# A graph network on one core: normalised nodes turned chunk by chunk, three PSUM banks for the sums of three edge loops, lane numbers in a bank

## The chip, the cores and the metric

One core of a Trainium2 chip runs the whole program in one launch. The metric is the device time of that launch in microseconds, median of several executions. Engines are written as in the profile: PE multiplies matrices (PEld loads its weights), DVE and ACT work on whole tiles, POOL issues the indirect gathers and scatters here, SP issues the plain transfers.

## The reference

A graph of N = 6250 nodes with 128 features and E = 100,000 edges (`src` to `dst`, sorted by `dst`) goes through four layers, each followed by a residual and a layer norm:

```python
x = layernorm(x + conv(x))         # silu(h[src] + edge_attr @ we.T + be) summed by dst, silu, graph norm
x = layernorm(x + attend(x))       # h = x@W+b; e = leaky_relu(a_src.h[src] + a_dst.h[dst]); softmax over
                                   # all edges; weight * h[dst] summed by src
x = layernorm(x + heads(x))        # 8 heads of 16: clip(K[src].Q[dst]/4, -5, 5), exp, softmax per dst,
                                   # V[src] * weight summed by dst
x = layernorm(x + update(x))       # relu([x[src], x[dst], edge_attr] @ w1 + b1) @ w2 + b2 summed by dst,
                                   # then an MLP of [x, sum] with 256 hidden
```

Everything is float32.

## The kernel before, in words

Nodes lie as 50 tiles of 128 (NT; 49 of them, RT, hold real nodes), edges as tiles of 128. Since edges are sorted by `dst`, the edge tiles are walked in 832 steps of one edge tile and one node tile each; a step's sum by `dst` is a matmul with a one-hot matrix (edge by place in the node tile), and what an edge takes from its `dst` node is a matmul with that matrix transposed. What it takes from its `src` node is gathered from a table in DRAM by POOL, one indirect transfer for 128 edges.

The program is a row of stages, each a block in which every engine has its own instruction stream, written by hand. PSUM is one tile of 8 banks of 128x512 floats (`k.psum[:, bank, :]`). `pipeline(eng, iters, per, *stages, lags=...)` (line 79) emits an engine's loop: stage s of turn t - lag(s), one after the other, so the order of the names is the order of issue on the engine.

*conv* (`phase_conv_edges`, 585): not touched. DVE's comparison of line 705 to 708 reads its lane numbers from PSUM.

*Node stages.* Three stages begin with a layer norm of all nodes and a linear layer on it. `Norm` (494) does it in three cuts of tiles, 12, 20 and 18: DVE makes a cut's input (`make`), takes statistics (`count`, `moments`), ACT takes the root (`scalar_root`), DVE finishes (`finish`), then 4, 6 and 10 tiles of the cut are scaled by DVE (`apply`, 538) and the rest by ACT (`scalar_apply`, 550). `Linear` (401) takes chunks of 4 tiles (3 in place): PE turns a chunk (line 435), once all scaling of its cut is done on both engines, ACT copies it out (456), PE multiplies (442), DVE adds the bias into the result (472, or 474 with a scale), SP stores it in the table in DRAM (480). Products of at most `RING = 3` chunks are under way. In heads there are two layers on the same turned nodes, key and value (256 columns, 13 chunks) and query (128 columns); in relation also two, source and target (256 columns each). POOL's gathers begin when the first one's table is stored.

*Place* (`phase_place`, 852) has 104 groups of 8 steps, two buffers (j). Per group ACT makes |lo - p| (`distance`, 997) and from it the one-hot `is_lo` (`is_nought`, 1002); DVE makes `is_rel` by a comparison (`matrices`, 1082, line 1085) and a mask (`make_mask`, 1087). PE ranks the edges (`place`), scores them (`score`, 963 and 964) and fetches their rows of H (`expand`, 968, line 973) into banks 4 + 2j + h, 4 of the 8 steps each. ACT copies those to SBUF (1012). POOL scatters each step's rows into the DRAM table by_src (1157).

*Heads* (`phase_heads`, 1300) has 208 groups of 4 steps. POOL gathers key and value rows (1352) when DVE has staged the indices (`stage`, 1424). ACT makes the transposed one-hot (1393 to 1405), PE expands the query (`expand`, 1364), DVE multiplies with the key (1453), sums by head (1463), clips (1466). ACT takes the exponential into 8 columns of the message tile (`weigh`, 1408, line 1412), DVE multiplies the value rows by it (`messages`, 1470, line 1472) and stages the next indices. PE sums (`sum_into_nodes`, 1375, line 1381) with the one-hot of `sum_matrix` (1447, line 1449: lane numbers in PSUM bank 7) and DVE adds the sums into the nodes (1491).

*Relation* (`phase_relation`, 1499) has 208 groups of 4 steps. POOL gathers (1568), PE makes the hidden layer in banks 0 to 3 (`hidden_product`, 1582, lines 1590 and 1591), DVE adds the gathered rows in two halves (`add_rows`, line 1680) and stages the next indices, ACT takes Relu (1631), PE sums into banks 4 to 7 (`sum_into_nodes`, 1596, line 1602) with the one-hot that DVE makes in two comparisons (`sum_matrix`, 1666, line 1669: lane numbers in SBUF), DVE adds the four sums (`add_sums`, 1691, line 1701). The bank of a sum is 4 + 2(j mod 2) + q // 2. PE's order is hidden product of a group, sum of two groups back. DVE's order and the bank formula are:

```python
sums = lambda j, q: k.psum[:, 4 + 2 * (j % 2) + q // 2, (q % 2) * HID:(q % 2 + 1) * HID]
pipeline(v, ITERS, GROUPS, add_sums(0), sum_matrix, add_sums(1), add_rows(0), add_sums(2),
         add_rows(1), add_sums(3), lags=(3, 1, 3, 1, 3, 1, 3), loads=3)
```

The stage *attend* between place and heads and the stage *update* after relation are not touched (update has a norm of its own making with other code).

## Time and profile before

| | |
|---|---|
| median of 3 runs | 6345.29 us (6343.44 to 6368.28) |
| profiled execution | 6365.66 us, span 6363.8 us |
| TensorE clock granted, mean of the span | 0.742 of full speed |
| PE, PEld | 4055.2 us busy (64%), 3547.0 (56%) |
| DVE | 2974.2 us (47%) |
| ACT | 1648.3 us (26%) |
| POOL | 3414.5 us (54%) |
| HBM | 554.38 MB read, 89.82 MB written, 101 GB/s over the span |

The stages in the profiled execution, in us from the span's start: tables to 91, conv's loop 91 to 1408, graph norm and place's node stage to 1524, place's loop 1524 to 2890, attend to 3183, heads' node stage 3183 to 3272 (its key and value part to 3242), heads' loop to 4685, relation's node stage to 4793, relation's loop to 6224, update to the end. A busy share is an average over these stages, so the prediction reads each by itself. An entry such as "[7.13 <-remote]" behind an instruction is the idle time of its engine just before it and what ended that time: a line of another engine, "issue" where the profile shows nothing that was waited for, or "remote" for a semaphore that did not come from an engine's instruction in the records next to it.

### The profile page before, as it was taken

How to read it: one execution, taken by the hardware profiler on the slowest of the kernel's cores; microseconds unless marked ns; L12 is line 12 of the kernel's file. 1: busy time of each engine (PE TensorE's matmuls, PEld its weight loads, DVE VectorE, ACT ScalarE, POOL GpSimd, SP SyncE). 2: the span in 40 equal slices, each digit the busy share in tenths (PEclk: the TensorE clock that was granted, in tenths of full speed). 3: DMA queues.
4: the chain of work that ended last, by engine and by line, in shares of the span. 5: the costliest groups of instructions: out<-in, count | busy, mean ns of one | idle time of the engine just before them, and what ended most of it. 6: DMA issues, size and time to landing. Idle time of an engine off the chain costs nothing. (4 is left out here: it accounts for less than half of the span.)

```text
span 6363.8 us, 91532 instructions
## 1 busy us (share of the span) xinstructions
PE 4055.2 (64%) x19917; PEld 3547.0 (56%) x19918; DVE 2974.2 (47%) x8069; ACT 1648.3 (26%) x2977; POOL 3414.5 (54%) x3536
## 2 busy tenths in 40 slices
PE   4444444456888888787844333344458888888887
PEld 3444444445777777776743333344346677667765
DVE  5444444455333333336755555455464444445455
ACT  0111111113222222226732222222223333333331
POOL 3655555542566656566635555555524555555550
PEclk6766766775555555558977777766678999999999
DMA  4322222235222222226633333333324444444441
GB/s 103 85 81 81 80 79 79 80 77 99 80 80 83 82 79 81 80 74 183 194 99 97 95 98 95 97 95 95 98 93 121 132 132 133 133 136 137 130 131 49
DMA packets 491156, 645.54 MB, mean 101 GB/s; under 512 B 94519, under 2 KB 354059, under 8 KB 490798
## 3 DMA queue, kind: packets, MB, share of 16 engines
q1 hardware_dynamic: 346462, 312.02, 18.0%
q0 software_dynamic: 132032, 325.99, 17.7%
q10 hardware_dynamic: 12560, 6.52, 0.7%
q14 instruction: 82, 0.67, 0.0%
q8 instruction: 20, 0.33, 0.0%
HBM read 554.38 MB, written 89.82 MB: 101 GB/s over the span
## 5 line engine op out<-in xcount | busy, mean ns | idle before, releaser
L1568 POOL DMA_INDIRECT R<-table_ps,r_idx x832 | 805.5, 968 | 730.4 <-DVE r_idx L1642 393.1
L1352 POOL DMA_INDIRECT R<-table_kv,h_idx x832 | 804.0, 966 | 693.5 <-DVE h_idx L1424 383.4
L1157 POOL DMA_INDIRECT by_src<-R,p_idx x832 | 825.1, 992 | 631.9 <-issue 245.7
L626 POOL DMA_INDIRECT R<-table,c_idx x784 | 747.4, 953 | 560.1 <-DVEq L721 284.8
L1381 PE MATMUL psum<-R,h_oh 128*128 128x137 f32 x1664 | 338.8, 363 | 809.8 <-DVE R L1491 745.7
L658 PE MATMUL psum<-R,c_oh 128*128 x1664 | 351.0, 376 | 691.4 <-remote 237.5
L1381 PEld LDWEIGHTS psum<-R,h_oh 128*128 128x128 f32 x1664 | 292.5, 254 | 840.2 <-DVE R L1491 759.9
L658 PEld LDWEIGHTS psum<-R,c_oh 128*128 128x128 f32 x1664 | 299.5, 270 | 740.8 <-issue 740.8
L1701 DVE TENSOR_TENSOR R<-R,psum 128x256 f32 x832 | 343.6, 413 | 727.8 <-remote 437.4
L1590 PE MATMUL psum<-w_L_gnn_re_w,r_ea 128*128 128x256 f32 x1664 | 549.2, 413 | 188.4 <-DVE X L1680 170.6
L973 PE MATMUL psum<-R 128*128 x1664 | 438.0, 426 | 183.4 <-issue 178.9
L1591 PE MATMUL psum<-R 128*128 x1664 | 537.3, 405 | 19.2 <-issue 19.1
L739 DVE TENSOR_TENSOR R<-R,psum 128x128 f32 x832 | 238.6, 287 | 577.3 <-remote 301.2
L973 PEld LDWEIGHTS psum<-R 128*128 128x128 f32 x1664 | 381.8, 323 | 222.6 <-issue 222.3
L1590 PEld LDWEIGHTS psum<-w_L_gnn_re_w,r_ea 128*128 128x128 f32 x1664 | 336.4, 207 | 273.2 <-issue 224.5
L963 PE MATMUL psum<-p_src_score,R 128*128 128x50 f32 x1664 | 467.9, 374 | 19.8 <-issue 19.5
L1602 PE MATMUL psum<-X,early_cols 128*128 128x256 f32 x1664 | 411.3, 389 | 18.6 <-issue 15.4
L668 ACT ACTIVATE R<-R 128x512 f32<-128x512 f32 x196 | 123.4, 629 | 1146.1 <-DVE R L717 885.5
L964 PE MATMUL psum<-R 128*128 x1664 | 399.2, 307 | 27.9 <-issue 27.4
L1631 ACT ACTIVATE X<-X 128x1024 f32<-128x1024 f32 x208 | 219.9, 1057 | 754.4 <-DVE X L1680 645.2
L963 PEld LDWEIGHTS psum<-p_src_score,R 128*128 128x128 f32 x1664 | 380.6, 280 | 51.4 <-issue 51.0
L964 PEld LDWEIGHTS psum<-R 128*128 128x128 f32 x1664 | 387.5, 285 | 20.1 <-issue 19.9
(338 smaller groups left out, 7440.5 us busy)
## 6 DMA issues: line engine op xcount, KB each, us to landing
R<-by_src SPq DMA_DIRECT2D x220, 260.0 KB, 3.1
r_ea<-in_ea_t SPq DMA_DIRECT2D x832, 64.0 KB
R<-in_ea_t SPq DMA_DIRECT2D x196, 256.0 KB
R<-rel_rows SPq DMA_DIRECT2D x104, 256.0 KB
R<-lo_rows SPq DMA_DIRECT2D x104, 256.0 KB
h_rel<-rel_rows SPq DMA_DIRECT2D x208, 128.0 KB
r_rel<-rel_rows SPq DMA_DIRECT2D x208, 128.0 KB
by_src<-R,p_idx POOLq DMA_INDIRECT x832
```

The costliest lines, as they stand in the source:

```text
L626: g.indirect_dma_start(out=rows[:, u, :], out_offset=None, in_=table, in_offset=bass.IndirectOffsetOnAxis(ap=idx[:, j // GROUPS % 2, u:u + ...
L658: mm = pe.matmul(k.psum[:, 2 + j % 2, q * D:(q + 1) * D], oh[:, j % 2, q, :], ring[:, bass.ds(regs["slot"][G * (j % GROUPS) + q], 1), :], ...
L963: pe.matmul(cols[:, 0:NT], is_lo[:, j, q * P:(q + 1) * P], src_score[:], start=True, stop=True)
L964: mm = pe.matmul(cols[:, NT:WIDE], is_rel[:, j, q * P:(q + 1) * P], H[:, bass.ds(regs["node"][G8 * j + q], 1), D + 1:D + 2], start=True, s ...
L973: mm = pe.matmul(k.psum[:, 4 + 2 * j + h, (q % G) * D:(q % G + 1) * D], is_rel[:, j, q * P:(q + 1) * P], H[:, bass.ds(regs["node"][G8 * j ...
L1157: g.indirect_dma_start(out=by_src, out_offset=bass.IndirectOffsetOnAxis(ap=idx[:, u:u + 1], axis=0), in_=rows[:, u, :], in_offset=None).th ...
L1352: g.indirect_dma_start(out=rows[:, u, :], out_offset=None, in_=table, in_offset=bass.IndirectOffsetOnAxis(ap=idx[:, u:u + 1], axis=0)).the ...
L1381: mm = pe.matmul(sums(j, q), oh[:, j % 2, q, :], msg[:, j % 2, q, :], start=True, stop=True)
L1568: g.indirect_dma_start(out=rows[:, u, :], out_offset=None, in_=table, in_offset=bass.IndirectOffsetOnAxis(ap=idx[:, u:u + 1], axis=0)).the ...
L1590: pe.matmul(hidden(j, q), ea[:, G * j + q, :], k.w["L3_gnn_re_w1"][:, 2 * HID:3 * HID], start=True, stop=False)
L1591: mm = pe.matmul(hidden(j, q), oht[:, j % 2, q * P:(q + 1) * P], Dh[:, bass.ds(regs["node"][G * j + q], 1), :], start=False, stop=True)
L1602: mm = pe.matmul(sums(j, q), oh[:, j % 2, q, :], msg[:, j % 2, q, :], start=True, stop=True)
```

## The change

It has five parts.

1. *Linear.* The ring of products under way is 6 banks divided by the banks of a chunk: 6 chunks in place and for the query, 3 elsewhere. Sums of the first `on_scalar` chunks can be plain copies by ACT (`scalar_moves`), counted by a semaphore of their own; whoever waits for a sum asks `wait_sums`. `sums` gives, for each point of DVE's order in the norm, up to which chunk it has made the sums.
2. *Norm.* Scaling goes by the linear layer's chunks: DVE takes 1 tile of each chunk in place and heads, 2 in relation, ACT the rest, and each signals per chunk; PE turns a chunk when that chunk is scaled. The cuts become 15, 21, 14 in place and 16, 20, 14 in relation (heads 12, 20, 18 as before). In relation ACT makes the first 7 sums of the source layer, whose bias is zero. `make` comes in two steps. DVE's sums start earlier in its order in place and heads.
3. *Place's loop.* ACT makes `is_rel` too, by the two activations it uses for `is_lo`; the distances of both have one buffer. `expand` has three banks: the first half of both j goes to bank 4, the second to 5 or 6; it waits for one more copy. Bank 7 holds lane numbers, set by one matmul, and the mask is made from it.
4. *Heads' loop.* The exponential is taken twice: into PSUM bank 6, from where the messages read it, and then into the message tile. Waits move with it.
5. *Relation's loop.* The sums have three banks: q = 0 and 1 of every group use bank 4, q = 2 and 3 bank 5 or 6; PE's sum waits for the first two adds of the group before. Bank 7 holds lane numbers, and each group has one comparison.

The core of the diff:

```diff
+        self.ring = 6 // self.banks
...
+    def wait_sums(self, eng, n):
+
+        if n < self.on_scalar:
+            eng.wait_ge(self.moved, n + 1)
+        else:
+            eng.wait_ge(self.added, n - self.on_scalar + 1)
...
-            pe.wait_ge(self.norm.done, self.norm.cut_of(at + t - 1) + 1)
-            pe.wait_ge(self.norm.scaled, self.norm.cut_of(at + t - 1) + 1)
+            pe.wait_ge(self.norm.scaled, n + 1)
+            if self.norm.on_vector:
+                pe.wait_ge(self.norm.done, n + 1)
...
-            if n >= self.RING:
-                pe.wait_ge(self.added, n - self.RING + 1)
+            if n >= self.ring:
+                self.wait_sums(pe, n - self.ring)
...
+    def scalar_moves(self, a, upto):
+        for n in range(self.scalar_sums, min(upto, self.on_scalar)):
+            first, t = self.chunks[n]
+            a.wait_ge(self.product, n + 1)
+            for at in range(0, t, self.fit):
+                m = min(self.fit, t - at)
+                ins = self.nc.scalar.copy(self.OUT[:, first + at:first + at + m, :],
+                                          self.k.psum[:, self.bank(n, at), 0:m * self.cols].rearrange("p (t d) -> p t d", d=self.cols))
+            ins.then_inc(self.moved, 1)
+            self.scalar_sums = n + 1
...
+        last = len(self.cuts) - 1
         for n, cut in enumerate(self.cuts):
+            make(cut, 0)
             if n:
                 self.finish(link, v, n - 1)
+                self.apply_chunks(v, Y, OUT, n - 1, linear)
+                linear.vector(v, sums[2 * n - 2])
+            make(cut, 1)
+            self.count(v, Y, cut.start, cut.stop).then_inc(self.counted, 1)
             self.moments(link, v, n)
-        self.finish(link, v, len(self.cuts) - 1)
+            if n:
+                linear.vector(v, sums[2 * n - 1])
...
+        for n, (at, t) in enumerate(linear.chunks):
+            if at in [cut.start for cut in self.cuts]:
+                self.scalar_root(a, self.cut_of(at))
+                linear.scalar_copies(a, n)
+                linear.scalar_moves(a, n - 1)
+                a.wait_ge(self.known, self.cut_of(at) + 1)
+            for tile in range(at + min(self.on_vector, t - 1), at + t):
+                ins = self.nc.scalar.activation(OUT[:, tile, :], Y[:, tile, :], ACT.Identity, bias=self.shift[:, tile:tile + 1],
+                                                scale=self.root[:, tile:tile + 1])
+            ins.then_inc(self.scaled, 1)
+            linear.scalar_copies(a, n)
+            linear.scalar_moves(a, n - 1)
+        linear.scalar_copies(a, linear.count)
+        linear.scalar_moves(a, linear.count)
...
+        norm = Norm(nc, c, sem, "n0_", (slice(0, 15), slice(15, 36), slice(36, NT)), 1)
...
+        expand_bank = lambda j, h: 4 + h * (1 + j)
...
-                        pe.wait_ge(rows_ready, 2 * n + h + 1)
+                        pe.wait_ge(rows_ready, 2 * n + 3 - h)
...
+                def distances(i, j):
+                    n = PER * i + j
                     a.wait_ge(lo_in[j], 16 * i + 16)
+                    a.wait_ge(lo_ready, n + PER)
+                    nc.scalar.activation(lo_away, lo[:, j, :], ACT.Abs, bias=k.minus_part[:, 0:1]).then_inc(lo_used, 1)
+                    a.wait_ge(rel_in[j], 16 * i + 16)
+                    if not (isinstance(n, int) and n < 1):
+                        a.wait_ge(rel_ready, n)
+                    nc.scalar.activation(rel_away, rel[:, j, :], ACT.Abs, bias=k.minus_part[:, 0:1]).then_inc(rel_used, 1)
+
...
-                def matrices(i, j):
-                    v.tensor_scalar(is_rel[:, j, :], rel[:, j, :], k.part[:, 0:1], None, ALU.is_equal).then_inc(rel_used, 1)
...
+                    pe.wait_ge(kept, n + 3)
...
+                    a.wait_ge(msg_ready, n + GROUPS)
+                    nc.scalar.activation(share, score[:, j % 2], ACT.Exp).then_inc(weighed, 1)
                     a.wait_ge(spread, n + 1)
-                    nc.scalar.activation(msg[:, j % 2, :, D:D + HEADS], score[:, j % 2], ACT.Exp).then_inc(weighed, 1)
+                    nc.scalar.activation(msg[:, j % 2, :, D:D + HEADS], score[:, j % 2], ACT.Exp).then_inc(kept, 1)
...
-                                    msg[:, j % 2, :, D:D + HEADS].unsqueeze(3).to_broadcast([P, G, HEADS, HD]),
+                                    share.unsqueeze(3).to_broadcast([P, G, HEADS, HD]),
...
-        sums = lambda j, q: k.psum[:, 4 + 2 * (j % 2) + q // 2, (q % 2) * HID:(q % 2 + 1) * HID]
+        sums = lambda j, q: k.psum[:, 4 + (q // 2) * (1 + j % 2), (q % 2) * HID:(q % 2 + 1) * HID]
+        lane, lane_set = k.psum[:, 7, 0:P], sem("lane_set")
...
-                    pe.wait_ge(added, G * n + G)
+                    pe.wait_ge(added, G * n + G + 2)
...
-                    for h in range(2):
-                        ins = v.tensor_tensor(oh[:, j % 2, 2 * h:2 * h + 2], k.lane[:].unsqueeze(1).to_broadcast([P, 2, P]),
-                                              k.rel_cols[:, bass.ds(i * U + G * j + 2 * h, 2)].unsqueeze(2).to_broadcast([P, 2, P]),
-                                              ALU.is_equal)
-                    ins.then_inc(oh_ready, 1)
+                    v.tensor_tensor(oh[:, j % 2], lane.unsqueeze(1).to_broadcast([P, G, P]),
+                                    k.rel_cols[:, bass.ds(i * U + G * j, G)].unsqueeze(2).to_broadcast([P, G, P]),
+                                    ALU.is_equal).then_inc(oh_ready, 1)
```

## Rows read from the trace of the kernel before

**Rows 1.** Stretches: length, busy PE, PEld, DVE, ACT, POOL (x instructions), clock, DMA, GB/s.

```profile
...
91.00:1408.00 1317.00, 621.07 (x3259) 571.03 (x3260) 564.29 (x1386) 139.19 (x208) 745.90 (x784) 0.69 0.28 78
1457.00:1515.00 58.00, 26.05 (x150) 24.79 (x150) 45.87 (x128) 20.67 (x51) 0.00 (x0) 0.62 0.80 131
1524.00:2890.00 1366.00, 1100.13 (x5170) 985.07 (x5169) 421.53 (x1243) 342.77 (x412) 825.13 (x832) 0.56 0.27 79
...
3183.00:3242.00 59.00, 35.73 (x152) 29.80 (x153) 45.24 (x133) 20.73 (x47) 0.00 (x0) 0.74 0.24 99
3272.00:4685.00 1413.00, 577.14 (x3328) 538.14 (x3328) 723.69 (x2080) 319.03 (x620) 788.81 (x816) 0.72 0.33 94
4689.00:4754.00 65.00, 36.78 (x151) 30.64 (x152) 48.97 (x129) 19.59 (x46) 0.00 (x0) 0.71 0.22 90
4793.00:6224.00 1431.00, 1204.90 (x4992) 1001.16 (x4992) 697.59 (x1870) 477.91 (x618) 790.40 (x816) 0.93 0.47 131
...
```

**Rows 2.** POOL's gathers and scatters by line: ns min/median/max, first and last start us.

```profile
...
L626 POOL DMA_INDIRECT R<-table,c_idx x784: 946/952/1657, 89.5 to 1359.1; - x196
...
L1157 POOL DMA_INDIRECT by_src<-R,p_idx x832: 963/969/1494, 1528.0 to 2886.3; - x167
...
L1352 POOL DMA_INDIRECT R<-table_kv,h_idx x832: 940/946/1512, 3247.0 to 4668.4; - x167
...
L1568 POOL DMA_INDIRECT R<-table_ps,r_idx x832: 940/946/1203, 4757.8 to 6204.2; - x167
...
```

**Rows 3.** Order of time around POOL's first gathers in heads: start, length, instruction, idle.

```profile
...
3241.75 11.21 PE L442 MATMUL psum<-w_L_gnn_Wq,R 128*128 128x128 f32 x98 [1.12 <-DVE R L472]
...
3246.98 1.02 POOL L1352 DMA_INDIRECT R<-table_kv,h_idx  x1 [75.16 <-issue]
...
3259.06 0.69 DVE L474 SCALAR_TENSOR_TENSOR R<-psum,b_L_gnn_bq 128x512 f32<-128x512 f32 x1 [7.13 <-remote]
...
3265.82 0.95 POOL L1352 DMA_INDIRECT R<-table_kv,h_idx  x1 [0.30 <-issue]
3269.64 0.89 DVE L474 SCALAR_TENSOR_TENSOR R<-psum,b_L_gnn_bq 128x512 f32<-128x512 f32 x2 [9.89 <-remote]
...
```

**Rows 4.** Who waited for whom, whole span: total us, times, longest.

```profile
...
DVE R L1701 <- remote: 437.4, 70, 10.4
...
```

**Rows 5.** Groups by line and shape: busy us, mean ns, idle before them, releasers.

```profile
...
L1669 DVE TENSOR_TENSOR early_cols<-lane,rel_cols 128x256 f32<-128x256 f32 x416 | 157.5, 420 | 0.2 <-issue 0.2
...
L1449 DVE TENSOR_TENSOR h_oh<-psum,rel_cols 128x512 f32<-128x512 f32 x208 | 142.4, 684 | 226.5 <-remote 162.4 <-PE psum L1381 42.8 <-issue 21.3
...
L997 ACT ACTIVATE R<-R,minus_part 128x1024 f32<-128x1024 bf16 x104 | 120.0, 1154 | 0.8 <-PE psum L442 0.8
...
L1012 ACT COPY R<-psum 128x512 f32<-128x512 f32 x208 | 119.1, 588 | 1011.3 <-remote 447.1 <-PE psum L973 416.1 <-issue 147.9
...
L1085 DVE TENSOR_SCALAR R<-R,part 128x1024 f32<-128x1024 bf16 x104 | 79.3, 762 | 154.1 <-ACT R L1012 77.2 <-issue 76.7
...
```

**Rows 6.** Order of time in the place loop, one gather beside line 1085.

```profile
...
2025.30 1.15 POOL L1157 DMA_INDIRECT by_src<-R,p_idx  x1 [6.29 <-DVE R L1137]
...
2025.57 0.75 DVE L1085 TENSOR_SCALAR R<-R,part 128x1024 f32<-128x1024 bf16 x1 [0.17 <-ACT R L1012]
...
```

**Rows 7.** Order of time in heads' node stage: the tail of the sums.

```profile
...
3222.23 3.78 PE L442 MATMUL psum<-w_kv,R 128*128 128x256 f32 x8 [3.77 <-ACT R L456]
...
3231.60 1.89 PE L442 MATMUL psum<-w_kv,R 128*128 128x256 f32 x8
...
3239.81 1.89 DVE L472 TENSOR_TENSOR R<-psum,b_kv 128x512 f32<-128x512 f32 x3 [0.66 <-PE psum L442]
...
```

**Rows 8.** Order of time in the relation loop, one group's sum and adds.

```profile
...
5559.35 0.59 PE L1602 MATMUL psum<-X,early_cols 128*128 128x256 f32 x2 [0.63 <-issue]
...
5562.16 0.41 DVE L1701 TENSOR_TENSOR R<-R,psum 128x256 f32 x1
...
5564.33 0.69 PE L1590 MATMUL psum<-w_L_gnn_re_w,r_ea 128*128 128x256 f32 x2 [2.10 <-DVE X L1680]
...
```

160 lines of the change are left out of this document (85 added, 75 removed).

## The prediction

> **What bounds the kernel now.** First the page's busy shares: no engine is full, so I cut the span into stages and read busy time in each [rows 1]. Four loops over groups of edges take 5,527 of 6,364 us. Per gather or scatter that POOL issues they cost 1317/784 = 1.68 us (conv), 1366/832 = 1.64 (place), 1413/832 = 1.70 (heads), 1431/832 = 1.72 (relation), with very different work beside them: PE is busy 1205 us in relation and 577 in heads. What they share is POOL's queue of indirect transfers. One takes 0.95 us with 0.30 before it [rows 2, 3], so 832 without a pause would be 1,040 us. The other 326 to 391 us (conv, by its 784: 337) are pauses. The timeline of heads shows what they are [rows 3]: POOL starts at 3246.98 and issues until 3266.77 with a short gap each. Meanwhile PE's 98 products of the query are over at 3252.96, yet DVE's sum of them waits 7.13 us for "remote" and starts at 3259.06, the next 9.89 us, until 3269.64, 2.9 us after POOL's run has ended. So while POOL issues on and on, other engines hear of finished work late. In the loops that ends as a cycle: a run of gathers, then a stall of all, since indices and buffers come free late. DVE's adds of the relation loop waited so 70 times, 437 us in all, 10.4 at most [rows 4]. I take it that a loop's length is POOL's busy time plus such stalls, and that a cheaper DVE or PE step moves it only in part.
>
> A second thing lengthens POOL's own part. The usual gather takes 0.946 us (0.969 in place), the longest 1.20 to 1.51 [rows 2]. By mean less median, [rows 1] over [rows 2], the excess is (825.13/832 - 0.969) x 832 = 19 us in place, (788.81/816 - 0.946) x 832 = 17 in heads, (790.40/816 - 0.946) x 832 = 19 in relation, and nothing in conv (745.90/784 = 0.951 against 0.952). In place the long ones lie across line 1085: 1.15 us at 2025.30, with the comparison running 2025.57 to 2026.32 [rows 6]. In heads and relation the candidates are lines 1472 and 1669, which read two SBUF tiles; conv's comparison reads its lane numbers in PSUM and harms nothing.
>
> **The change, part by part.**
> *Place loop.* The comparison of line 1085 (0.76 us x 104 = 79 us of DVE) goes; ACT makes the matrix with two more activations per group of 1.154 us, 104 x 2.31 = 240 us [rows 5]. ACT's turn becomes 4 x 1.154 + 2 x 0.588 = 5.8 of 13.1 us per group: covered by PE's own 1100/104 = 10.6, and if that cover is gone the price is what the second pair ends late. On ACT the copies queue behind the pair. The three banks of the expansion cost nothing while the copies follow within that turn. Gain: the 19 us of long scatters, at three quarters, since an end in a pause is not felt: **-14** (0 to -19).
> *Heads loop.* Exp is made twice, first into PSUM, from where the messages read it, then into the kept tile. The new instruction costs ACT at most its mean there, 319.03/620 = 0.51 us x 208 = 107, of 1,094 idle; the messages run meanwhile (0.68 us, as the comparison of that shape [rows 5]), so nothing on the path; uncovered it would be 107. Gain: three quarters of 17, **-13** (0 to -17).
> *Relation loop, comparison.* Two at 157.5/208 = 0.757 us per group become one as line 1449, 142.4/208 = 0.684 [rows 5]: 15 us of DVE, half of it felt, **-8** (0 to -15), and three quarters of the 19 of long gathers, **-14** (0 to -19).
> *Relation loop, banks.* The lane numbers take bank 7, so PE's sum of a group now also waits for the first two adds of the group before, which share bank 4. Queued behind it on PE is the next hidden product, for that wait DVE's rows, ACT's Relu and the stage of indices for POOL. Before, such a wait existed only two groups back, so the price must be bounded. Where all is in step the adds are long over: nothing, or a small gain of order, which no row supports, so 0 is the end. Where an add was late, as at 5562.16, the sum that began at 5559.35 would begin about 5562.6, 3.25 later [rows 8]; 70 such [rows 4] make 227. The hidden product there was waiting 2.10 us for DVE anyway [rows 8], which leaves 1.15 x 70 = 80, and PE has 226 us idle in this loop [rows 1]. I take **+29**, a bit over a third of the 80.
> *Node stages.* Each chunk of the normalised nodes is now turned as soon as it is scaled, not when its whole cut is; sums come earlier in DVE's order, place and query have six chunks under way instead of three, and in relation ACT makes seven of the sums as bare copies (0.588 each [rows 5]). The floor is DVE's busy time: 46 of 58 us in place, 45 of 59 in heads, 49 of 65 in relation [rows 1]. In heads the tail is PE at half clock (3.78 us for 8 products from 3222.23, 1.89 from 3231.60) after waiting 3.77 us for a copy, and then the sums, ending 3241.70 [rows 7]; with the sums drawn forward by one chunk the tail has about 3 chunks of 1.9 us less, bought with one slow one: **-6** (+2 to -14). Place has the same order with a shorter chain: **-8** (0 to -12). In relation seven of the sums leave DVE, but ACT then does scales, copies and moves in series, some 2.7 us a chunk: **-9** (+5 to -16). If ACT is late, PE's next turn is. SP stores each chunk in the old order, after whichever engine made it; POOL's queue gets nothing new in any stage.
> *Left alone:* tables, conv, attend, update. The lane product is one matmul per stage.
> Sum: -14 - 13 - 8 - 14 + 29 - 8 - 6 - 9 = **-43 us**. Against the profiled execution (span 6363.8, time 6365.66) that is 6,323; that execution is 20 us above the median of three, 6345.29, and on the median's scale it is **6,302**.
>
> A rule that speaks of this: in place POOL's scatter was 1.15 us beside line 1085 and 0.969 otherwise [rows 6, 2]. The Trainium skill, "SBUF — State Buffer", section "Who interferes with whom", has it that DVE in its two-port mode and GpSimd share an exclusively locked port pair, and that a DVE instruction with two SBUF inputs contends with GpSimd's reads. By that rule whoever holds the port blocks the other, so all of the 55 us would go and DVE would win too; by the rows I count three quarters and nothing for DVE. It makes the second rival below larger, no more.
>
> **The rivals.**
> *The pace is held by the stalls (0.26).* If a loop's length is set by how late signals come while POOL issues, then 0.03 us less per gather only makes the next stall start sooner. For it: the four loops cost the same per gather with very different work [rows 1], and conv, which has no long gathers, is no faster. Then only the node stages gain, -23: **6,322**.
> *The locks count in full and more (0.12).* All of 55 us, 15 for the comparison, no bank wait, node stages -30: **6,245**. Against it: conv again.
> *Bank 4 costs what it says (0.10), the other side.* PE's sum waits for the first two adds of the group before, each time DVE's adds are held up. If PE's delay hands on to the gathers, as it must where indices are staged behind it, the price is the 227 us and not 29: -72 + 227 = +155, **6,500**. For it: the adds wait 437 us [rows 4] in the very loop. Against: PE's next work waits for DVE anyway [rows 8]. It decides for "slower" from a price of 72 + 32 = 104 us on, half of the bound.
> *The clock (0.05).* In relation PE was granted 0.93, in heads, where it has many short pauses, 0.72 [rows 1]. If the new wait breaks PE's work into such pieces, 1205 us become 1205 x 0.93/0.72 = 1,556, 125 above the loop's 1431: 6,302 + 125 = **6,427**. The Trainium skill, "TensorE: Matmul & The Clock Gate", section "A second HAM failure mode: psum-queue depth-cycling", tells of a kernel that cycled through PSUM banks and idled briefly between groups of matmuls, and whose clock swung between its levels. The trace has the low level where PE has gaps, but shows no such case of banks.
>
> **How the numbers follow.** The forecast itself has 0.47; its own range is 6,267 to 6,353: below, half of the way to all the best ends together (-112); above, the banks at 80 and the rest as it is (+8). 0.5% is 32 us, about what a measurement of this kernel can tell from no change, so faster means under 6,314. Of the forecast's 0.47 I put 0.35 there, 0.11 within and 0.01 above 6,377; of the held pace 0.07 and 0.18, with 0.01 slower; the second rival's 0.12 is all faster; the third and fourth are slower, 0.15. Faster 0.54, same 0.29, slower 0.17. The range leaves out both slow rivals (0.15) and the best half of the second (0.05): 6,240 to 6,375.
>
> **What would show it.** Right: line 1669 once per group at about 0.68 us; POOL's mean gather within 0.01 of its median in place, heads and relation, and those three loops 13 to 25 us shorter; ACT in place at some 580 us busy; node stages ending 6 to 9 us after fewer. The banks' wait would stand as idle time of line 1602 released by DVE's line 1701; 30 us of growth in the relation loop or less confirms the term. Wrong: loops of the same length with means at the median (held pace); relation longer than 1,480 us with PE idle before 1602 (third rival), or with a granted clock below 0.85 (fourth). The forecast as a whole is wrong outside 6,240 to 6,375.

## The result, and the profile after

The changed kernel is slower by 1%: 6407.47 us median of 4 runs (6390.21 to 6438.22) against 6344.36 for the kernel before (4 runs beside it, 6332.1 to 6368.28), a ratio of 1.0096 with a 95% interval of 1.007 to 1.0122. The forecast was 6,302, faster, with a range of 6,240 to 6,375.

The page of the changed kernel: span, busy times, the 40 slices of POOL and clock, and the groups that matter (line engine op, out<-in, count | busy us, mean ns | idle before it and its releasers).

```profile
span 6393.2 us, 92216 instructions
PE 4045.8 (63%) x19921; PEld 3544.1 (55%) x19922; DVE 2876.9 (45%) x7738; ACT 1881.9 (29%) x3412; POOL 3362.6 (53%) x3536
...
L1626 POOL DMA_INDIRECT R<-table_ps,r_idx x832 | 787.4, 946 | 795.4 <-DVE r_idx L1701 485.0
L1400 POOL DMA_INDIRECT R<-table_kv,h_idx x832 | 787.3, 946 | 716.5 <-DVE h_idx L1476 408.5
L1204 POOL DMA_INDIRECT by_src<-R,p_idx x832 | 806.7, 970 | 647.6 <-ACT R L1060 277.9
...
L1762 DVE TENSOR_TENSOR R<-R,psum 128x256 f32 x832 | 342.9, 412 | 807.4 <-remote 632.4
L1661 PE MATMUL psum<-X,early_cols 128*128 128x256 f32 x1664 | 477.1, 437 | 261.6 <-DVE R L1762 249.3
```

POOL's transfers did what was forecast: in all three changed loops the mean is now the median, 0.946, 0.946 and 0.970 us, and 52 us of POOL's busy time are gone. Yet what POOL sits idle before them grew by more: 795.4 for 730.4 us in relation, 716.5 for 693.5 in heads, 647.6 for 631.9 in place. The last two rows show where it is new: PE now waits 249.3 us for line 1762, DVE's adds of the sums (1701 before), and those adds wait 632.4 us for "remote" instead of 437.4 [rows 4]. Before, PE's sums read:

```profile
L1602 PE MATMUL psum<-X,early_cols 128*128 128x256 f32 x1664 | 411.3, 389 | 18.6 <-issue 15.4 <-ACT X L1631 2.5
```

So they are also 66 us longer in PE's own time (437 ns each for 389), while the two rows of the hidden product fell by 55 us together (549.2 and 537.3 to 521.4 and 510.4). That fits the pause shown below, where the stretch at the lower clock falls on a sum.

The same by lines, POOL's transfers of place, heads and relation: ns min/median/max, then first and last start, which answer to [rows 2].

```profile
L1204 POOL DMA_INDIRECT by_src<-R,p_idx x832: 963/970/999, 1504.4 to 2867.3; - x167
...
L1400 POOL DMA_INDIRECT R<-table_kv,h_idx x832: 940/947/1017, 3219.6 to 4651.2; - x167
...
L1626 POOL DMA_INDIRECT R<-table_ps,r_idx x832: 940/947/959, 4725.1 to 6233.9; - x167
```

First to last start is the length of a loop, and from the last of one to the first of the next lies the node stage with what stands around it. From [rows 2]: place 1358 to 1363 us (+5), heads 1421 to 1432 (+10), relation 1446 to 1509 (+62). The stretches between fell: conv to place 168.9 to 161.5 (-7), place to heads 360.7 to 352.3 (-8), heads to relation 89.4 to 73.9 (-15). Conv's loop, which is not touched, fell by 15 in this one profile; with the other profiles below its length lies anywhere from 1254 to 1279, so a loop's length in one profile is good to some 10 us. The changed parts sum to +46 us; with conv's -15 that is the +29 between the two profiled spans (6363.8 and 6393.2). The medians differ by more, +63, since the profiled execution of before was 20 us above its median and that of the changed kernel 12 below.

Stretches of the changed kernel: length, busy PE, PEld, DVE, ACT, POOL, clock, DMA share, GB/s; they answer to [rows 1].

```profile
1504.00:2869.00 1365.00, 1065.78 (x5153) 962.73 (x5152) 349.46 (x1131) 540.85 (x615) 806.65 (x832) 0.56 0.26 79
3219.00:4653.00 1434.00, 587.77 (x3362) 549.05 (x3360) 718.77 (x2057) 354.13 (x830) 787.28 (x832) 0.71 0.34 95
4725.00:6253.00 1528.00, 1240.92 (x5076) 1031.96 (x5074) 695.26 (x1685) 487.42 (x625) 787.36 (x832) 0.91 0.45 126
```

DVE is 70 us less busy in place, ACT 200 more, and the clock is what it was in place and heads (0.56, 0.71) and 0.91 for 0.93 in relation. The fullest engine of each loop is no nearer to full than before; the loops are longer because POOL pauses more.

What a pause looks like now, in order of time in the relation loop: start, length, instruction, [idle before it <- what ended it].

```profile
5561.54 0.94 POOL L1626 DMA_INDIRECT R<-table_ps,r_idx  x1 [0.30 <-issue]
...
5564.45 0.42 DVE L1762 TENSOR_TENSOR R<-R,psum 128x256 f32 x1 [8.32 <-remote]
5565.39 0.41 DVE L1762 TENSOR_TENSOR R<-R,psum 128x256 f32 x1
...
5565.86 3.78 PE L1661 MATMUL psum<-X,early_cols 128*128 128x256 f32 x8 [4.64 <-DVE R L1762]
...
5567.25 0.16 DVE L1701 CAST r_idx<-src_cols 128x4 int32 x1
...
5568.27 0.95 POOL L1626 DMA_INDIRECT R<-table_ps,r_idx  x1 [5.79 <-DVE r_idx L1701]
...
5569.89 0.42 DVE L1762 TENSOR_TENSOR R<-R,psum 128x256 f32 x1 [2.17 <-PE psum L1661]
...
5572.69 0.28 DVE L1701 CAST r_idx<-src_cols 128x4 int32 x1
```

POOL stops at 5562.48 for want of indices. Two microseconds later DVE hears of a sum it has waited 8.32 us for, and makes its first two adds. Only now may PE make the next sum (5565.86, 4.64 us idle, released by line 1762), in 3.78 us at half clock (granted 0.50 from 5565.8 to 5569.7), and the adds of that sum wait another 2.17 us. Before, that sum would have been made while DVE was still waiting, as the one at 5559.35 was [rows 8]. This pause is hardly longer for it: its indices were staged at 5567.25, before the late sum was done. The next group's are: DVE staged them at 5572.69, 5.4 us later, behind the adds that had waited for the sum. Before, the same two stagings stood 3.5 us apart (5564.03 and 5567.52).

**Pauses counted.** I call a pause a gap of over 2 us between the end of one of POOL's transfers and the start of the next in the same loop. A loop is then its transfers + short gaps (0.31 to 0.38 us each on average) + pauses. The table has, for conv, place, heads and relation, us from the first start to the last end, and in brackets number x mean length of the pauses. The kernels of the second and third block were run elsewhere or later and are told of below.

```
                   conv               place              heads              relation
before             1270.6 (58x4.64)   1359.2 (59x4.91)   1422.3 (67x5.66)   1447.4 (81x4.63)
after              1255.4 (51x4.66)   1364.0 (70x4.52)   1432.5 (67x6.05)   1509.8 (98x4.87)
rel_old            1270.3 (53x4.88)   1363.6 (71x4.47)   1435.1 (67x6.08)   1436.7 (83x4.44)
rel_banks          1273.5 (55x4.87)   1371.4 (69x4.65)   1433.4 (67x6.06)   1491.7 (93x4.72)
rel_one            1263.4 (55x4.63)   1357.6 (72x4.44)   1428.1 (68x5.94)   1481.5 (79x5.32)
rel_late           1264.1 (53x4.67)   1361.2 (69x4.56)   1431.3 (67x6.01)   1496.2 (100x4.79)

p_nodes            1279.8 (62x4.27)   1375.5 (65x4.69)   1437.3 (67x5.92)   1466.9 (90x4.53)
p_no_heads         1262.0 (60x3.96)   1393.1 (71x4.92)   1438.7 (67x5.94)   1478.9 (86x4.77)
p_no_place         1274.2 (63x4.19)   1369.7 (65x4.74)   1469.7 (68x6.55)   1474.4 (87x4.73)

nodes_alone         985.5 (none)      1081.2 (none)      1062.5 (none)      1084.2 (1x7.17)
nodes_and_place     985.5 (none)      1059.6 (none)      1063.5 (none)      1085.1 (1x7.82)
after_rel_old       985.4 (none)      1059.7 (none)      1040.0 (none)      1084.8 (1x7.67)
after_again         985.5 (none)      1059.7 (none)      1040.2 (none)      1082.3 (1x6.27)
parts               985.1 (none)      1070.3 (none)      1067.1 (none)      1084.9 (1x7.62)
```

From before to after the pauses grew by 26 us in place, 26 in heads and 102 in relation, more than the transfers and short gaps gave back. Between two pauses POOL issues whole groups of four in relation. Before, 45 of these runs were of 8 gathers, 28 of 12 and 8 of 16 or 20; in the changed kernel 90 are of 8 and 8 of 12 or 16 (in `rel_banks` 80 and 14, in `rel_old` 52 and 32). The loop has more pauses because POOL now seldom gets a third group before it must stop.

### The profile page after: what moved, and what is told of

The parts are those of the page before. It is cut to its first block and busy times, and to the rows that moved or that the text cites. A ratio compares the mean times of both kernels' runs of the same rounds, so it can differ in the third digit from the quotient of the medians.

```text
span 6393.2 us, 92216 instructions
## 1 busy us (share of the span) xinstructions
PE 4045.8 (63%) x19921; PEld 3544.1 (55%) x19922; DVE 2876.9 (45%) x7738; ACT 1881.9 (29%) x3412; POOL 3362.6 (53%) x3536
## 3 DMA queue, kind: packets, MB, share of 16 engines
q0 software_dynamic: 132032, 325.99, 17.5%
## 5 line engine op out<-in xcount | busy, mean ns | idle before, releaser
L1626 POOL DMA_INDIRECT R<-table_ps,r_idx x832 | 787.4, 946 | 795.4 <-DVE r_idx L1701 485.0
L1400 POOL DMA_INDIRECT R<-table_kv,h_idx x832 | 787.3, 946 | 716.5 <-DVE h_idx L1476 408.5
L1204 POOL DMA_INDIRECT by_src<-R,p_idx x832 | 806.7, 970 | 647.6 <-ACT R L1060 277.9
L1762 DVE TENSOR_TENSOR R<-R,psum 128x256 f32 x832 | 342.9, 412 | 807.4 <-remote 632.4
L1661 PE MATMUL psum<-X,early_cols 128*128 128x256 f32 x1664 | 477.1, 437 | 261.6 <-DVE R L1762 249.3
L1011 PE MATMUL psum<-R 128*128 x1664 | 422.4, 424 | 225.5 <-issue 224.3
L1661 PEld LDWEIGHTS psum<-X,early_cols 128*128 128x128 f32 x1664 | 352.6, 217 | 356.0 <-DVE R L1762 279.3
L1649 PE MATMUL psum<-w_L_gnn_re_w,r_ea 128*128 128x256 f32 x1664 | 521.4, 396 | 6.6 <-issue 6.5
L1011 PEld LDWEIGHTS psum<-R 128*128 128x128 f32 x1664 | 378.3, 325 | 259.8 <-issue 259.7
L1650 PE MATMUL psum<-R 128*128 x1664 | 510.4, 389 | 6.6 <-issue 6.5
L1002 PE MATMUL psum<-R 128*128 x1664 | 390.7, 302 | 35.4 <-issue 34.4
L1150 DVE TENSOR_TENSOR R<-psum,R 128x408 f32<-128x408 f32 x104 | 60.6, 583 | 742.1 <-remote 516.6
```

Of the source, the lines that this page charges most:

```text
L1002: mm = pe.matmul(cols[:, NT:WIDE], is_rel[:, j, q * P:(q + 1) * P], H[:, bass.ds(regs["node"][G8 * j + q], 1), D + 1:D + 2], start=True, s ...
L1011: mm = pe.matmul(k.psum[:, expand_bank(j, h), (q % G) * D:(q % G + 1) * D], is_rel[:, j, q * P:(q + 1) * P], H[:, bass.ds(regs["node"][G8 ...
L1204: g.indirect_dma_start(out=by_src, out_offset=bass.IndirectOffsetOnAxis(ap=idx[:, u:u + 1], axis=0), in_=rows[:, u, :], in_offset=None).th ...
L1400: g.indirect_dma_start(out=rows[:, u, :], out_offset=None, in_=table, in_offset=bass.IndirectOffsetOnAxis(ap=idx[:, u:u + 1], axis=0)).the ...
L1626: g.indirect_dma_start(out=rows[:, u, :], out_offset=None, in_=table, in_offset=bass.IndirectOffsetOnAxis(ap=idx[:, u:u + 1], axis=0)).the ...
L1649: pe.matmul(hidden(j, q), ea[:, G * j + q, :], k.w["L3_gnn_re_w1"][:, 2 * HID:3 * HID], start=True, stop=False)
```

## The experiments

The theories at the outset: **A**, the relation loop grew because PE's sum waits for bank 4; **B**, it grew because of the comparison, or of POOL's new pace.

### The relation loop taken apart

`rel_old` is the changed kernel with the relation loop of before:

```diff
-        sums = lambda j, q: k.psum[:, 4 + (q // 2) * (1 + j % 2), ...]
+        sums = lambda j, q: k.psum[:, 4 + 2 * (j % 2) + q // 2, ...]
-                    pe.wait_ge(added, G * n + G + 2)
+                    pe.wait_ge(added, G * n + G)
-                    v.tensor_tensor(oh[:, j % 2], lane..., ALU.is_equal)            # PSUM, 128x512
+                    for h in range(2): v.tensor_tensor(..., k.lane..., ALU.is_equal) # SBUF, 128x256
```

> The changed kernel with the relation loop as it was before: sums in four banks, two comparisons with lane numbers from SBUF, no wait for the adds of the group before. Everything else stays changed. Theory A (PE's wait for bank 4 made the loop longer): from POOL's first to its last gather in relation about 1446 us as before (the changed kernel 1509), the kernel some 60 us faster than the changed one, near 6,345, same as before or up to 0.5% faster. Theory B (the longer loop is a matter of the new pace of POOL without long gathers, or of what the earlier stages leave behind): the loop stays above 1490 with PE not waiting for DVE before its sums, or the kernel stays within 15 us of the changed one.

Measured: 6333.66 us, 0.9979 of before (0.9959 to 1.0), 74 us under the changed kernel; the relation loop has 1437 us and 83 pauses. The growth over before is in this loop's edits.

`rel_banks` keeps the three banks and the wait and takes only the comparison back.

> The changed kernel with the comparison alone taken back: three banks for the sums and PE's added wait stay, but two comparisons read the lane numbers in SBUF. Theory A: PE's wait is all of it, so the relation loop is as long as in the changed kernel, 1509 us, or up to 19 us longer, since POOL's mean gather is back at 0.968 us. Theory B (the lane numbers in PSUM or the one wide comparison do it): the loop is back near 1446.

Measured: 6390.46 us, 1.007 of before (1.0046 to 1.0093), 17 us under the changed kernel. The loop has 1492 us: 55 longer than with four banks, with everything else the same, and PE waits 235 us for line 1760, DVE's adds, in 77 stalls. So the wait costs 55 us (57 by the medians of `rel_banks` and `rel_old`, which ran side by side). With both edits the loop is 18 us longer still; the intervals of the two ratios overlap, so that this rest is real isn't shown.

`rel_one` is the reverse: four banks, no wait, one comparison of 128x512 with its lane numbers in SBUF.

> The changed kernel with four banks for the sums and no added wait, but one comparison of 128x512 per group, its lane numbers in SBUF. Against the kernel with the whole relation loop taken back it shows the one comparison by itself: 0.075 us less DVE work per group, 15 us. My forecast counted half of that, 8 us. Theory A says the same as that kernel within 10 us. POOL's long gathers stay, since both inputs are in SBUF: mean 0.968 us or somewhat more.

Measured: 6374.23 us, 1.0038 of before (1.0018 to 1.0059), 41 us over `rel_old`; the loop has 1481 us, 45 more. This went against A's "the same within 10 us" and against my own 8 us of gain: DVE does its comparison 0.073 us a group cheaper and the loop is longer. POOL's transfers in it, and for comparison those of `rel_old`:

```profile
L1625 POOL DMA_INDIRECT R<-table_ps,r_idx x832 | 823.2, 989 | 731.6 <-DVE r_idx L1699 441.8 <-issue 289.9
```

```profile
L1625 POOL DMA_INDIRECT R<-table_ps,r_idx x832 | 807.1, 970 | 703.0 <-DVE r_idx L1699 381.7 <-issue 317.3 <-DVE X L1739 4.0
```

One comparison of 0.684 us with two SBUF inputs holds a gather up for longer than two of 0.757 together do (mean 0.989 for 0.970, longest 1.463 for 1.207): 16 us of the 45. The wait for indices is 60 us longer in exchange for shorter small gaps (238 us of them for 261), and there are as many pauses but of 5.32 us, not 4.44. Why one wide instruction makes longer pauses than two narrow ones these runs don't say.

`rel_late` puts PE's wait for bank 4 in the middle of the four steps:

```diff
-                    pe.wait_ge(added, G * n + G + 2)
-                    for q in range(G):
+                    pe.wait_ge(added, G * n + G)
+                    for q in (2, 3, 0, 1):
+                        if q == 0:
+                            pe.wait_ge(added, G * n + G + 2)
                         mm = pe.matmul(sums(j, q), oh[:, j % 2, q, :], msg[:, j % 2, q, :], start=True, stop=True)
```

> The changed kernel with PE's sums in another order: steps 2 and 3, whose banks 5 and 6 are free, come first, and the wait for the first two adds of the group before stands between them and steps 0 and 1. If the wait for bank 4 is the cause, the two products of about 0.6 to 1.2 us hide a part of each of the 91 stalls (249 us of idle time, 2.7 on average, in the changed kernel): idle time before the sums' line down by 60 us or more, the loop 15 to 40 us shorter than 1509. If the cause lies elsewhere, no difference beyond 5 us.

Measured: 6393.44 us, 1.0085 of before (1.0057 to 1.0112). PE's idle time for the adds fell from 249 to 205 us (91 and 89 stalls), the loop from 1510 to 1496, with 100 pauses. A had said 60 us or more and 15 to 40: the idle time fell by 44 and the loop by 14, which is little beside the scatter of some 10, and the ratio's interval overlaps the changed kernel's. The direction fits A, the size doesn't show it, and the number of pauses did not fall. Perhaps half the product hidden does not help when DVE adds only after all four steps; no run tests that.

### A second surprise: where the pauses are absent

Next came the changed kernel without one or more of its parts, to split place and heads. `nodes_only` has all three loops as before, `no_heads` the heads and relation loops as before, `no_place` the place and relation loops as before (their parts of the diff above taken back, word for word). `pace` is `nodes_only` with

```diff
-                            g.wait_ge(msg_ready, GROUPS * i + u // G + 1)            # heads
+                            g.wait_ge(msg_ready, GROUPS * i + u // G + 3)
-                            g.wait_ge(summed, 2 * (GROUPS * i + u // G) + 2)         # relation
+                            g.wait_ge(summed, 2 * (GROUPS * i + u // G) + 6)
```

> The changed kernel with all three edge loops as before: of the change only the node stages are left. In the changed kernel's trace the time between POOL's last transfer of one loop and its first of the next fell by 7 us ahead of place, 8 ahead of heads and 15 ahead of relation. If these belong to the node stages alone, this kernel is some 31 us faster than before, near 6,318, faster than the one that kept the place and heads loops changed (6,334). If they depend on the loops ahead of them, or a loop that starts earlier ends no earlier, the gain is under 15.

> Node stages and the place loop changed, heads and relation loops as before. Theory D (pace: a shorter gather only makes POOL's next pause start sooner): putting back the long gathers of heads costs nothing, the heads loop from first to last gather goes from 1432 back to about 1421 us and POOL's pauses from 6.05 us on average to 5.66, since the second exponential is gone too. Theory E (each long gather lay on the path, and the second exponential costs nothing): the loop gets 17 us longer than 1432.

> Node stages and the heads loop changed, place and relation loops as before. Theory D: the place loop from first to last scatter stays within 8 us of the 1363 of the changed kernel although POOL's scatters take 19 us more in all. Theory E: it gets 19 us longer. By the changed kernel's trace POOL waits for ACT's copies 278 us there, 200 before, so a third way is that ACT's longer turn took the gain, and the loop is some 5 us shorter without it.

> As the kernel with the node stages alone changed, but POOL is held closer: in heads a group's gathers wait until the messages two groups back are done instead of four, in relation until both adds two groups back are done instead of four. Nothing else differs, so this changes POOL's runs alone. Theory F (a pause of POOL has a fixed price of 4.5 to 5 us, because other engines hear late of finished work while it issues, and what changes a loop's length is how many pauses there are): runs become 8 gathers where they were 12, there are about 100 pauses instead of 67 and 81, each still over 4 us, and the loops grow by 50 us or more, relation to about 1,500 as with three banks. Theory G (the pauses are what the other engines' work takes, and they shrink when there are more of them): both loops stay within 20 us of before.

Measured: 5033.04, 5014.23, 5010.86 and 6006.39 us, with the kernel *before* at 5062.44 beside them (7 runs, 5059.96 to 5065.27). The same kernel before, unchanged, takes 6,344 us in one group of runs and 5,062 in another. The ratios are 0.9939 (0.9923 to 0.9956), 0.9903 (0.9887 to 0.992), 0.9899 (0.9882 to 0.9915) and 1.1865 (1.1846 to 1.1885). The profiles of the first three say what differs (the kernel before has no profile there): POOL issues the 784 or 832 transfers of a loop without a pause, but for one of 7 to 8 us in relation. Everything I had tried to find out about pauses was not there to be found, so D to G stayed untested, and `pace` only shows what its own wait does: in heads 206 pauses of 5.10 us and a loop of 2033 us, in relation, with the same two groups under way instead of four, 1095 for 1085. Relation has much room in that respect, heads none, and POOL can be made to pause there too.

So a second group asked what the whole change does there.

> The changed kernel as it is, run beside the others of this group. The last group of kernels ran where the kernel before takes 5,062 us and POOL issues its transfers with no pause at all in the four loops, while in the first group it took 6,349 with pauses of 4.5 to 6 us after each 8 to 16. Where there are pauses (before near 6,345): 1% slower than before, as measured, with about 98 pauses in relation. Where there are none (before near 5,062): POOL alone sets the loops, every long gather lay on the path, and the change is faster by the node stages (31 us), 18 in place, 20 in heads and 20 to 40 in relation, unless the wait for bank 4 makes PE the later one: 4,950 to 4,990.

> The changed kernel with the relation loop as before. Where POOL pauses: 60 to 75 us faster than the changed kernel. Where it does not: 20 to 40 us slower than the changed kernel, since long gathers come back (1084 us from first to last gather against some 1050), so the sign of this part of the change turns with the pauses.

> Node stages and the place loop changed, heads and relation loops as before. Where POOL pauses: the heads loop is 1421 us from first to last gather as before, against 1432 changed. Where it does not: 20 us slower than with the heads loop changed, 1060 to 1066 us against 1039.

> The node stages alone. Some 30 us faster than before wherever it runs: it was 29.4 us in medians without pauses. Where POOL pauses the place loop is about 1358 us from first to last scatter, against 1363 changed, so this kernel is then the fastest of the group or even with the two others that have the old relation loop.

Measured, before at 5061.19 us: the changed kernel 4987.74, a ratio of 0.9854 (0.9838 to 0.9871), **1.5% faster**; with the old relation loop 4988.81 (0.9858), where I had expected 20 to 40 us more; with nodes and place 5012.4 (0.9905); nodes alone 5034.79 (0.9947). Stretches of `after_again` (conv, place, heads, relation; columns as above):

```profile
82.00:1070.00 988.00, 580.25 (x3130) 533.45 (x3130) 553.29 (x1319) 138.08 (x207) 746.74 (x784) 0.75 0.38 105
1220.00:2280.00 1060.00, 969.69 (x5158) 887.07 (x5157) 344.85 (x1135) 536.50 (x616) 805.48 (x831) 0.62 0.34 102
2633.00:3675.00 1042.00, 650.66 (x3377) 590.61 (x3375) 724.39 (x2068) 340.06 (x832) 787.02 (x832) 0.74 0.45 131
3743.00:4828.00 1085.00, 1082.93 (x5018) 952.89 (x5017) 684.19 (x1657) 482.61 (x622) 786.80 (x832) 1.00 0.65 177
```

POOL's busy time is the same as with pauses (805, 787, 787), and a loop is 832 x (0.946 + 0.304) = 1,040 us in heads, which is all of it. There the long transfers lay on the path in full: place 1081.2 to 1059.7 us, heads 1062.5 to 1040.2, which is 21.5 and 22.3 us, and POOL's busy time fell by 20.7 and 22.3. Relation gains 2 us of the 29 that its gathers got shorter: PE is busy 1082.93 of 1085 us at clock 1.00 and is the bound. For the same reason neither the bank wait nor the wide comparison costs anything: PE's sums waited for DVE's adds 2.9 us there, in 2 stalls, for 249.3 in 91. My forecast of 20 to 40 us for relation missed that.

The difference between the two places can be seen at one spot, the query's sums while POOL's first gathers of heads go out. With pauses (changed kernel):

```profile
3213.94 11.21 PE L452 MATMUL psum<-w_L_gnn_Wq,R 128*128 128x128 f32 x98 [1.11 <-DVE R L490]
...
3219.64 1.02 POOL L1400 DMA_INDIRECT R<-table_kv,h_idx  x1 [71.30 <-issue]
...
3233.16 0.69 DVE L492 SCALAR_TENSOR_TENSOR R<-psum,b_L_gnn_bq 128x512 f32<-128x512 f32 x1 [7.85 <-remote]
...
3236.66 0.29 DVE L492 SCALAR_TENSOR_TENSOR R<-psum,b_L_gnn_bq 128x128 f32<-128x128 f32 x1 [2.81 <-remote]
```

and without (`after_again`, the same kernel):

```profile
2633.99 1.02 POOL L1400 DMA_INDIRECT R<-table_kv,h_idx  x1 [71.67 <-issue]
...
2638.87 0.69 DVE L492 SCALAR_TENSOR_TENSOR R<-psum,b_L_gnn_bq 128x512 f32<-128x512 f32 x1 [0.20 <-PE psum L452]
...
2639.77 0.89 DVE L492 SCALAR_TENSOR_TENSOR R<-psum,b_L_gnn_bq 128x512 f32<-128x512 f32 x2 [0.20 <-PE psum L452]
```

In the second, DVE walks through its sums at 0.89 us each though POOL issues all the time; in the first it stops 7.85 us, until 3233.16, though PE's last product was over at 3225.15. I take this late news to be what starts the pauses. Waits that end in "remote" sum to between 2,636 and 3,317 us over all engines but PEld in each of the nine traces with pauses, and to nothing in the other eleven. `pace` is one of those eleven: its 206 pauses in heads bring no such wait, so pauses alone don't make news late. That late news makes the pauses is argued from the order of time and not tested by itself. What makes it late in one place and not in the other no run here shows; instructions, transfers and their lengths are the same. It isn't slower packets: those of POOL's queue took 17.5% of the 6393 us of all 16 DMA engines with pauses and 23.1% of 4986 without, 1,119 and 1,152 us.

### Place and heads where POOL pauses

The same three kernels, now where POOL does pause; the kernel before took 6432.43 us beside them (25 runs, 6410.55 to 6469.77).

> The node stages alone, asked for again because the two groups that had it ran where POOL never pauses. Where POOL pauses (before near 6,345): Theory D (pace) says 31 us faster than before, about 6,316, and as fast as with the place and heads loops changed (0.9979 of before), or faster. Theory E (each long gather lay on the path there too) says 36 us slower than that kernel. Where POOL does not pause: 0.995 of before again.

> Node stages and the place loop changed. Where POOL pauses: the heads loop 1421 us from first to last gather with 67 pauses of 5.66 us, as before, against 1432 with 67 of 6.05 when it is changed; in time within 10 us of the kernel with the node stages alone. Where it does not: 0.990 of before again.

> Node stages and the heads loop changed. Where POOL pauses: the place loop 1358 us with some 59 pauses, against 1363 with 70 when it is changed; the heads loop stays at 1432. Where it does not: 0.990 of before again.

Measured: the node stages alone 6401.75, 0.9949 of before (0.993 to 0.9968); with place changed 6415.85, 0.9973 (0.9949 to 0.9997); with heads changed 6443.24, 1.0011 (0.9987 to 1.0034). In the table above the place loop is 1393 us changed, 1370 and 1376 as before; the heads loop 1470 changed, 1437 and 1439 as before. By the medians the change costs 14 us in place and 41 in heads, by the loops 20 and 32. Both theories fall, E (a gain of 17 and 19) clearly, but D's plain form too: the gathers' gain isn't just swallowed, the loops get longer. In heads there are still 67 or 68 pauses, each 0.4 to 0.6 us longer, and the row that grew is DVE's comparison of line 1449. In `p_nodes` and `p_no_place`:

```profile
L1487 DVE TENSOR_TENSOR h_oh<-psum,rel_cols 128x512 f32<-128x512 f32 x208 | 142.6, 686 | 393.3 <-remote 371.7 <-issue 19.2 <-PE psum L1418 2.4
```

```profile
L1492 DVE TENSOR_TENSOR h_oh<-psum,rel_cols 128x512 f32<-128x512 f32 x208 | 142.5, 685 | 583.0 <-remote 500.6 <-issue 80.8 <-PE psum L1420 1.6
```

It waits 190 us more in all for PE's sum two groups back. That is not the edit's price: with the heads loop untouched the same row has 226.5 us in the kernel before [rows 5] and 393.3 in `p_nodes`. Two waits are new in `p_no_place`. PE's sum waits for the second exponential (36.9 us in 3 stalls), and ACT's first one waits until DVE's messages of the group before have read the one buffer of `share` (217.6 us in 108). In place POOL waits for ACT's copies 259 us in `p_no_heads` for 230 and 237 in the other two. Which of these lengthens a loop is argued, not shown. With the old relation loop but place and heads changed, the first group had 0.9979 of before, where these three would make it about 1.0035 (0.9973 + 1.0011 - 0.9949); the two groups differ by more than their intervals, so the sizes for place and heads are a range: 5 to 20 us and 10 to 40.

The last group was to say which edit it is:

```diff
-        share = k.psum[:, 6, 0:G * HEADS].rearrange("p (q h) -> p q h", q=G)
+        share = sb("share", [P, G, HEADS], F32)[:]
-        expand_bank = lambda j, h: 4 + h * (1 + j)                # place
+        expand_bank = lambda j, h: 4 + 2 * j + h
-                        pe.wait_ge(rows_ready, 2 * n + 3 - h)
+                        pe.wait_ge(rows_ready, 2 * n + h + 1)
-        lane = k.psum[:, 7, 0:P]
+        lane = k.lane
```

> Relation loop as before; place and heads loops changed but for the PSUM banks: in place ACT makes both one-hot matrices, but the expansion has its four banks and waits as before and the mask's lane numbers are in SBUF; in heads the exponential is taken twice with the new waits, but its first copy is in SBUF, so the messages read two SBUF tiles and the long gathers should be back. Where POOL pauses, for the heads loop: if the second exponential and its waits made it longer (1437 to 1469 us in one group, 1421 to 1432 in the other), it is as long as changed although the gathers are long again; if the shorter gathers turned into longer pauses, it is back at the old length. For the place loop: if the shared bank cost the 20 us (1371 to 1392), the loop is back near 1372 or below, with short scatters; if ACT's longer turn did, it stays near 1392. Where POOL does not pause: heads 1061 us, place 1059.

> Node stages, place and heads loops changed in full, relation loop as before, beside the other two. Where POOL pauses: by the last group the place loop is some 20 us and the heads loop 10 to 30 us longer than with the node stages alone, so this kernel is 30 us or more slower than that one and about even with before. By the first group, where it was 0.9979 of before, it is only 15 slower. Where POOL does not pause: 0.986 of before.

> The node stages alone, as the base of this group: 0.995 of before in either case.

It ran where nothing pauses (before 5062.76; 5030.95, 4991.95 and 5040.62 us, ratios of 0.9936, 0.9859 and 0.9955), so that question stays open. What it does show is what made the transfers long. With share in SBUF the heads loop is back at 1067 us (1040 with it in PSUM, 1064 in `q_nodes`): all of that gain comes from where the second input of line 1527 lies, and none from the order or the waits. In place 1070 lies halfway between 1060 and 1081: moving line 1085's comparison to ACT brought 11 us and the mask's lane numbers in PSUM the other 11, though my forecast had put all of it on line 1085. POOL's busy time says the same, for `q_nodes`, `parts` and `q_both_loops`: 826.9, 816.9 and 805.7 us in place, 810.8, 814.0 and 786.8 in heads.

## Why the prediction was wrong

**The long transfers, 41 us of gain forecast.** That they would vanish was right (mean and median differ by under 0.001 us), and so was whom I blamed in heads and relation. "At three quarters, since an end in a pause is not felt" is a term that failed. Where POOL pauses nothing of it arrives: the place loop is 5 to 20 us longer and the heads loop 10 to 40. Where it does not, all of it arrives in place and heads (21.5 and 22.3 us) and 2 of 29 in relation, where PE is full. The first rival, the pace held by the stalls, had the mechanism for place and heads; it lacked that the loops get longer. That the same edits add links (ACT's second pair, the second exponential and the one buffer it is read from) to what must be heard of before POOL can go on is my reading, and that cause stays open. As for the port rule of the Trainium skill, "SBUF — State Buffer", section "Who interferes with whom": both of its cases are in these rows, the two-port mode (line 1085) and two SBUF inputs against POOL (lines 1472, 1669 and the mask of 1090). The transfers' lengths agree with it: up to 1.49 us in place and 1.51 in heads before, at most 1.00 and 1.02 after. The rule speaks of POOL's instruction, and only where POOL is the bound is that the loop's time.

**The banks, 29 us of cost forecast.** It is 55 (`rel_banks` against `rel_old`). The bounds of 0 and 227 held, and 55 lies half-way between what I took and the middle bound of 80. The step "PE has 226 us idle in this loop, a bit over a third of the 80" failed: that idle time isn't spread. Of the 235 us that PE idles between POOL's first and last gather in the kernel before, 196 lie inside POOL's pauses, where the late adds are too. The new wait falls just where nothing covers it, and it shows in the count of pauses, 93 for 83.

**The comparison, 8 us of gain forecast.** Sign wrong: +45 us with four banks and lane numbers in SBUF (41 by the medians, 16 of it longer gathers); on top of three banks +18, within the scatter. That a cheaper instruction of an engine that is half idle gains half of its difference was an assumption without a row.

**The node stages, 23 us forecast.** 31 by the profile (7, 8 and 15 for 8, 6 and 9), and by the medians 31 in `p_nodes`, 29, 26 and 22 in `nodes_only`, `nodes_alone` and `q_nodes`. Right, and the one part that gains in either place; relation was under-sized.

**The rivals.** The third (bank 4, slower) had the right mechanism, its sign came (relation over 1,480 us, PE idle before its sums), and it gave 6,500. That the measured 6,407 is half-way from the forecast to it is chance: of its 227 us only 55 were felt, and the rest of the way is made of the comparison and of place and heads, +5 and +10 us in that profile for -14 and -13. The fourth did not happen: the clock in relation is 0.91 in the changed kernel for 0.93, and 1.00 without pauses. The chance of 0.17 for "slower" was too low mostly for one reason: four edits inside loops, whose rhythm I had called a cycle of stalls, were all priced as sums of instruction times. One reading was loose as well: the 1.68 to 1.72 us per transfer divided stretches of the timeline, and by POOL's own first to last they are 1.62, 1.63, 1.71 and 1.74, so the loops are less alike than I said. And the point I could not see from one profile is that the sign itself depends on whether that cycle is there: 1.0096 with it, 0.9854 without.

Where POOL pauses the best measured is the node stages alone (0.9949 there, 0.9947 without pauses), though its interval overlaps that of `rel_old`; where it does not, the change in full or with the old relation loop (0.9854, 0.9858). With the old relation loop it is at least not slower than before in either: 0.9979 and 0.9858.

## What to carry to other kernels

When loops with very different work cost the same per transfer and the waits read "remote", count the pauses of the engine that issues, and price an edit by whether it adds a link to what must be heard of before that engine goes on, not by the time of the instruction. Share a buffer only where its last reader is early in the stalled case, not in the average one. Time a change on more than one occasion, with the old kernel beside it: here the old kernel itself differs by 20%, and with it the sign.

## What the runs showed of the hardware that was not expected

- The kernel before took 6,344 and 6,349, 6,432, and 5,061 to 5,063 us in different groups of runs, each steady within 1%. The kernel before was profiled only in the first; there it has 265 pauses of over 2 us among POOL's 3,280 transfers, and the kernels of the other traces with pauses have 274 or more, of 4 to 6.5 us on average. Those without have one (`pace` apart), with the same median of 0.946 us for a gather. The record numbers the chip 0 for the runs of the table's first block behind `after` and also for the first two groups without pauses, 6 for the second block and 13 for `parts`; whether one number is one chip it doesn't say.
- Conv's loop, the same in all kernels, is 985 to 988 us without pauses, and 1255 to 1280 with them.
- A gather beside a comparison with two SBUF inputs of 0.684 us took up to 1.463 us, beside one of half the width up to 1.207, and with one of the inputs in PSUM 0.965 at most (all in relation).
